# A two-stage layer on one core: expert choice ahead of two routers, the other two as row products on ScalarE and GpSimd

## The reference

```python
x = x + xattn(layernorm(x), fside, ctx)     # per batch: int8-like linear 512->512, silu(gate) * up, linear 256->512
xn = layernorm(x)                           # 2048 tokens
logits = xn @ gate_w.T                      # 8 experts
_, sel = top_k(logits.sum(axis=0), 2)       # two experts for ALL tokens
rw = softmax(logits[:, sel], axis=1)        # a pair of weights for each token
h = gelu(einsum('nd,kdf->knf', xn, w1[sel]) + b1[sel])
y = einsum('knf,kfd->knd', h, w2[sel]) + b2[sel]
x = x + einsum('nk,knd->nd', rw, y)
```

## Time and profile before

| | |
|---|---|
| runs | 820.04, 821.65, 822.15 us (median 821.65) |
| span of the profiled execution | 818.7 us (what lies around it isn't in the profile; the median is 2.95 above the span) |
| PE busy | 771.5 us, 94% |
| DVE, ACT, POOL busy | 477.7, 354.6, 449.7 us |
| chain that ended last | PE 83%, POOL 8%, DVE 3% |
| mean granted clock of TensorE | 0.979 of full |

### The profile page before, as it was taken

The page is one execution under the profiler, slowest core; times in us unless marked ns, Lnnn a source line. Parts: engine busy times, 40 slices in busy tenths (PEclk is TensorE's granted clock), DMA queues, the critical chain, the costliest instruction groups (busy, mean ns, idle before and its releaser), DMA issues.

```text
span 818.7 us, 11342 instructions
## 1 busy us (share of the span) xinstructions
PE 771.5 (94%) x3570; PEld 624.1 (76%) x3577; DVE 477.7 (58%) x669; ACT 354.6 (43%) x660; POOL 449.7 (55%) x497
## 2 busy tenths in 40 slices
PE   5688666999999999999999999999999999999998
PEld 4666455688788888888888888888888888888886
DVE  5999759797754545454545454545454545454545
ACT  3967588743442434343424343434343434242422
POOL 1789997157564646464646464646464646464622
PEclk9899968999999999999999999999999999999999
DMA  9400000301010101010101010101010101010022
GB/s 344 173 2 1 1 0 2 129 1 51 1 52 1 51 0 49 3 50 2 48 4 51 1 45 6 42 9 44 7 41 11 36 15 36 15 32 19 0 103 104
DMA packets 19077, 32.34 MB, mean 39 GB/s; under 512 B 872, under 2 KB 11240, under 8 KB 18160
## 3 DMA queue, kind: packets, MB, share of 16 engines
q1 hardware_dynamic: 18896, 31.98, 11.1%
q10 hardware_dynamic: 160, 0.08, 0.0%
HBM read 27.87 MB, written 4.19 MB: 39 GB/s over the span
## 4 chain that ended last, share of the span: by engine, by line
PE 83%; POOL 8%; DVE 3%; issue 2%; ACT 2%; DMA 1%; ACTq 0%; POOLq 0%; DVEq 0%
PE slot L805 42%; PE slot L792 34%; PE slot L850 3%; POOL wv L366 2%; POOL xf L383 1%; PE slot L667 1%; POOL wv L372 1%; POOL cv L366 1%; PE slot L585 1%; DVE rmax L1226 1%; DMA b_rows<-in_L_ffn_b 1%; POOL rstd L340 1%; POOL h_lo L476 1%; DVE stats L1217 1%; DVE peak_x L1226 1%
## 5 line engine op out<-in xcount | busy, mean ns | idle before, releaser
L792 PE MATMUL slot<-xo,a_hi 128*128 128x512 f32 x840 | 259.1, 390 | 0.0
L1541 DVE SCALAR_TENSOR_TENSOR res<-slot,rw,res 128x512 f32<-128x512 f32 x256 | 178.5, 750 | 130.3 <-PE slot L805 130.2
L1570 DVE TENSOR_TENSOR e<-slot,e 128x512 f32<-128x512 f32 x150 | 103.8, 692 | 173.4 <-PE slot L792 173.3
L805 PE MATMUL slot<-w_hi,h_hi 128*128 128x512 f32 x512 | 201.3, 393 | 0.4 <-POOL h_lo L476 0.4
L805 PE MATMUL slot<-w_lo,h_hi 128*128 128x512 f32 x512 | 199.6, 390 | 0.0
L805 PE MATMUL slot<-w_hi,h_lo 128*128 128x512 f32 x512 | 199.4, 390 | 0.0
L792 PEld LDWEIGHTS slot<-xo,a_hi 128*128 128x128 f32 x840 | 157.4, 188 | 33.3 <-DVE e L1570 0.2
L476 POOL TENSOR_TENSOR h_lo<-e,h_hi 128x512 fp32r<-128x512 f32 x96 | 138.1, 1451 | 55.0 <-ACT e L1104 54.0
L792 PE MATMUL slot<-xo,a_lo 128*128 128x512 f32 x420 | 163.7, 390 | 0.0
L805 PEld LDWEIGHTS slot<-w_hi,h_hi 128*128 128x128 f32 x512 | 96.1, 188 | 25.1 <-POOL h_lo L476 5.6
L476 POOL TENSOR_TENSOR h_lo<-hid,h_hi 128x512 fp32r<-128x512 f32 x32 | 44.1, 1378 | 124.7 <-ACT hid L1104 124.7
(11 more groups left out here) (145 smaller groups left out, 814.5 us busy)
## 6 DMA issues: line engine op xcount, KB each, us to landing
raw<-in_L_ffn_w SPq DMA_DIRECT2D x32, 512.0 KB, 3.4
res<-in_x SPq DMA_DIRECT2D x4, 1024.0 KB, 11.9
wv<-in_fside_BxS2xS SPq DMA_DIRECT2D x4, 1024.0 KB, 12.8
out_x<-res SPq DMA_DIRECT2D x3, 1024.0 KB, 3.9
cv<-in_ctx SPq DMA_DIRECT2D x4, 512.0 KB, 13.1
out_x<-res SPq DMA_DIRECT2D x4, 256.0 KB, 2.7
b_row<-in_L_ffn_b SPq DMA_DIRECT2D x2, 256.0 KB, 4.6
b_rows<-in_L_ffn_b ACTq DMA_DIRECT2D x1, 64.0 KB, 6.0
```

Source lines behind the costliest of these rows:

```text
L792: last = t.matmul(dst, a[:, i, k, :], xo[tp][:, v, k, :], start=(start and n == 0), stop=(n == 3 * H - 1), skip_group_check=True)
L805: last = t.matmul(y_bank[j][:, :], a[:, i, j * P:(j + 1) * P], v[:, f, :], start=(start and n == 0), stop=(not start and n == 2), skip_gro ...
L1541: v.scalar_tensor_tensor(out=r, in0=y_bank[j][:, :], scalar=rw[:, ds(p, 1), n:n + 1].rearrange("p a b -> p (a b)"), in1=r, op0=ALU.mult, o ...
L1570: v.tensor_tensor(dst[:, :], src, other[:, :], ALU.add).then_inc(comb_ready, 1)
```

## The change

Names: T2L and T4L are areas of the tokens' operand tiles that are free at that time; `dot_product(j)` is a 128x512 piece of them.

- The routers of batches 2 and 3 are dropped from PE, with their copies and columns. In their place ACT writes 8 rows of normalised tokens (`dot_row`, 128 tokens x 512 features each), POOL multiplies each with the difference of the two chosen gate rows, which it has made from two rows loaded by DMA (`gate_difference`, `router_products`), and ACT sums each product into a column of `ldiff` with its accumulator (`dot_sum`).
- `expert_sums` comes before the routers of batches 1 and 0. The first up tile comes before the logit columns.
- The logit difference is picked at once, with one product instead of two. The power, its sum with 1 (now on POOL) and the token weights are made in two parts, one for each half.
- The first weights come by two DMAs, and a tile's low weight products come last in each pair of blocks.
- The work around pair 0 on DVE, ACT and POOL is put in another order.

```diff
--- before.py
+++ after.py
@@ -241,6 +249,9 @@
         hid_ready, h_ready = sem("hid_ready"), sem("h_ready")
         y_ready, y_free = sem("y_ready"), sem("y_free")
         stored = sem("stored")
+
+        def dot_product(j):
+            return part(1, (T2L, T4L)[j // 2])[:, (j % 2) * D:(j % 2) * D + D]
 
         x_bank, p_bank, w_bank, y_bank = bank[0], bank[1], bank[2], bank[4:8]
...
-            load_w1(0)
+            first = w1_v[ds(expert[0], 1), 0].rearrange("e p k f -> (e p) k f")
+            sp.dma_start(raw1[:, 0:H, :], first[:, 0:H, :]).then_inc(raw1_top, 16)
+            sp.dma_start(raw1[:, H:KD, :], first[:, H:KD, :]).then_inc(raw1_load, 16)
             load_w2(0)
             expert.append(value_of(1))
+            for k in range(TOPK):
+                sp.dma_start(gate_row[:, k, :], gate_w[ds(expert[k], 1), :].to_broadcast([P, D])).then_inc(gate_load, 16)
...
-            first_pair()
+            def gate_difference():
+                pool.wait_ge(gate_load, 16 * TOPK)
+                link(g.tensor_tensor(gate_row[:, 0, :], gate_row[:, 0, :], gate_row[:, 1, :], ALU.subtract))
+
+            def router_products(b):
+                for j in range(TT):
+                    pool.wait_ge(dot_rows, (b - B // 2) * TT + j + 1)
+                    g.tensor_tensor(dot_product(j), dot_product(j), gate_row[:, 0, :], ALU.mult).then_inc(dot_ready, 1)
+
+            def token_power(tp):
+                pool.wait_ge(lsub_ready, tp + 1)
+                at = slice(tp * HALF, tp * HALF + HALF)
+                link(g.tensor_tensor(lpow[:, at], euler[:, at], lsub[:, at], ALU.pow))
+                g.tensor_scalar(lden[:, at], lpow[:, at], 1.0, None, ALU.add).then_inc(lexp_ready, 1)
+
+            hid_lo(0, 0, 0)
+            token_power(0)
+            hid_lo(0, 0, 1)
+            hid_lo(0, 0, 2)
+            hid_lo(0, 0, 3)
+            gate_difference()
+            router_products(2)
+            router_products(3)
+            hid_lo(0, 1, 0)
+            weight_sums(0)
+            hid_lo(0, 1, 1)
+            token_power(1)
+            hid_lo(0, 1, 2)
+            hid_lo(0, 1, 3)
+            for i in range(7):
+                weight_lo(0, i)
+            down_lo(0, 0, 1)
+            down_lo(0, 1, 0)
...
@@ -774,11 +807,9 @@
             normed2(2, 1)
             normed2(3, 0)
             normed2(3, 1)
+            expert_sums()
             router(1)
-            expert_sums()
             router(0)
-            router(2)
-            router(3)
...
                     if q == 0:
-                        pe.wait_ge(a_ops_ready, 2 * f + h + 1)
+                        pe.wait_ge(a_hi_ready, 2 * f + h + 1)
                     pe.wait_ge(lo_ready[b], h + 1)
                     hi, lo = HI_AT[s][h], LO_AT[s][h]
-                    for k in range(H):
-                        for a, v in ((a_hi, hi), (a_hi, lo), (a_lo, hi)):
+                    for a, v in ((a_hi, hi), (a_hi, lo), (a_lo, hi)):
+                        if q == 0 and a is a_lo:
+                            pe.wait_ge(a_ops_ready, 2 * f + h + 1)
+                        for k in range(H):
                             last = t.matmul(TILE_BANK[n], a[:, 2 * f + h, k, :], xo[q][:, v, k, :],
                                             start=(m == 0), stop=(m == 3 * KD - 1))
                             m += 1
                 last.then_inc(prod_done, 1 if n < 3 else 4)
...
+            up_tile(0, 0)
+            logit_columns(1)
+            logit_columns(0)
+            up_tile(0, 1)
+            up_tile(0, 2)
+            up_tile(0, 3)
+            first_downs(0)
+            for n in range(4):
+                up_tile(1, n)
+            first_downs(1)
+            pe.wait_ge(hid_ready, 8 + 16)
...
@@ -998,8 +1038,11 @@
                 if lo == 0:
                     act.sem_inc(hid_ready, 8)
                     act.sem_inc(e1_ready, 2)
-                    act.wait_ge(raw1_load, 16)
                 for i in range(lo, hi):
+                    if i == 0:
+                        act.wait_ge(raw1_top, 16)
+                    if i == 1:
+                        act.wait_ge(raw1_load, 16)
                     plain_hi(i)
...
@@ -1084,39 +1127,46 @@
             keep_full(2, 0)
             keep_full(3, 0)
             keep_summed(2, 1)
+            keep_summed(3, 1)
             keep_hi(2, 0)
             keep_hi(2, 1)
-            keep_summed(3, 1)
             keep_hi(3, 0)
-            keep_hi(3, 1)
-            keep_logits(0)
             keep_logits(1)
             first_weights(0, 2)
+            keep_logits(0)
             first_weights(2, 4)
             s.activation(gelu_warm[:, :], half[:, 0:1], ACT.Gelu_apprx_tanh)
-            keep_logits(2)
-            keep_logits(3)
-            first_down_weights()
...
+            def dot_sum(b, j):
+                n = b * TT + j
+                act.wait_ge(dot_ready, n - NT // 2 + 1)
+                s.activation(dot_product(j), dot_product(j), ACT.Identity,
+                             accum_out=ldiff[:, n:n + 1]).then_inc(dot_summed, 1)
+
+            def dot_row(b, j):
+                act.wait_ge(nmr_ready[b], 2)
+                if b == B - 1:
+                    act.wait_ge(dot_summed, j + 1)
+                s.activation(dot_product(j), res[:, b * TT + j, :], ACT.Identity, bias=nmr[1][b][:, j:j + 1],
+                             scale=rstd[1][b][:, j:j + 1]).then_inc(dot_rows, 1)
...
-            first_pair()
+            first_bias()
+            gelu_tile(0, 0)
+            first_down_weights()
+            keep_hi(3, 1)
+            gelu_tile(0, 1)
+            gelu_tile(0, 2)
+            gelu_tile(0, 3)
+            dot_row(2, 0)
+            dot_row(2, 1)
+            dot_row(2, 2)
+            dot_row(2, 3)
+            dot_sum(2, 0)
+            dot_row(3, 0)
+            dot_sum(2, 1)
+            dot_row(3, 1)
+            dot_sum(2, 2)
+            dot_row(3, 2)
+            dot_sum(2, 3)
+            dot_row(3, 3)
+            dot_sum(3, 0)
+            dot_sum(3, 1)
+            dot_sum(3, 2)
+            dot_sum(3, 3)
+            gelu_tile(1, 0)
+            operand_hi(0, (T2H, T2L), 4)
+            gelu_tile(1, 1)
+            operand_hi(0, (T3H, T3L), 4)
+            gelu_tile(1, 2)
+            operand_hi(0, (T1H, T1L), 4)
+            gelu_tile(1, 3)
+            operand_hi(0, (T4H, T4L), 4)
+            later_weights()
...
+                dve.wait_ge(logcol_ps, 2)
+                cols = bank[3][:, 0:NT * E].rearrange("p (n e) -> p n e", e=2 * E)
+                link(v.tensor_tensor(between[:, :], onehot[:, 0, :], onehot[:, 1, :], ALU.subtract))
+                link(v.tensor_tensor(picked[:, 0:NT // 2, :], cols,
+                                     between[:, :].unsqueeze(1).to_broadcast([P, NT // 2, 2 * E]), ALU.mult))
+                link(v.tensor_reduce(ldiff[:, 0:NT // 2], picked[:, 0:NT // 2, :], AX.X, ALU.add))
+
+            def logit_maxima(tp):
+                at = slice(tp * HALF, tp * HALF + HALF)
+                v.tensor_scalar(is_top[:, 0, at], ldiff[:, at], 0.0, None, ALU.is_ge)
+                v.tensor_scalar(is_top[:, 1, at], ldiff[:, at], 0.0, None, ALU.is_le)
+                v.scalar_tensor_tensor(out=lsub[:, at], in0=ldiff[:, at], scalar=-1.0, in1=ldiff[:, at],
+                                       op0=ALU.mult, op1=ALU.min).then_inc(lsub_ready, 1)
...
             moments(3, 2)
-            keep_lo(0, 0)
+            normalise_last()
             keep_lo(1, 0)
-            normalise_last()
             token_sums(2)
-            keep_lo(1, 1)
             token_sums(3)
             token_total()
+            keep_lo(1, 1)
+            choose_experts()
+            keep_lo(0, 0)
             keep_lo(0, 1)
-            choose_experts()
-            keep_lo(2, 0)
-            keep_lo(2, 1)
-            keep_lo(3, 0)
-            keep_lo(3, 1)
+            pick_experts()
+            pick_bias()
             first_weights(0, 2)
             first_weights(2, 4)
-            pick_experts()
-            pick_bias()
-            first_down_weights()
+            keep_lo(2, 0)
             pick_logits()
-
-            def token_weights():
-                dve.wait_ge(lexp_ready, 1)
+            logit_maxima(0)
+            keep_lo(2, 1)
-            first_pair()
+            first_down_weights()
+            keep_lo(3, 0)
+            token_weights(0)
+            keep_lo(3, 1)
+            last_operands(0)
+            fourth_operand(0)
+            outputs_of(0, 0, 0)
+            middle_operands(0, 3)
+            outputs_of(0, 0, 1)
+            middle_operands(0, 4)
+            operand_lo(0, 0)
+            operand_lo(0, 1)
+            dve.wait_ge(dot_summed, 2 * TT)
+            logit_maxima(1)
+            operand_lo(0, 2)
+            token_weights(1)
+            outputs_of(0, 1, 0)
+            operand_lo(0, 3)
+            last_operands(1)
+            outputs_of(0, 1, 1)
+            fourth_operand(1)
```

(75 more changed lines are left out.)

70 lines of the change are left out of this document (24 added, 46 removed), and 8 rows, old and new, of the table SLOT_USES.

## The result

The changed kernel takes 830.89 us (median of 4 runs, 829.60 to 832.47) beside 820.99 us before (4 runs on the same chip, 820.04 to 822.15): a ratio of 1.0129, 95% interval 1.0107 to 1.0152. It is slower by about 1.3%. The profiled execution has a span of 827.7 us, 9.0 us more than before.

A forecast was written before the change was run, and what follows sets the result against it. PE was taken to bound the kernel, busy 94% of 818.7 us. 2.1 us won at the start, 11.0 of new PE waits, + 0.3 and - 0.2 gave + 9.0: span 827.7, median 830.7 us, range 822.5 to 835.5.

The forecast's parts named there:

- The sum: Whole kernel: - 2.1 + 11.0 + 0.3 - 0.2 = + 9.0 us of span, to 827.7; 2.95 carried over gives 830.7.
- The start: Up to the fourth up tile's end: two routers and half the logit columns off PE, 2.1 us won (1.0 to 3.5).
- The clock term: At the start: PE's clock 0.50 at the sums, rising during the routers, so 16 passes take 5.1 us.
- The chain of six steps: From the fourth up tile's end (163.7) through ACT, POOL and DVE to the combine freeing the Strassen bank, at 211.4 us.
- step 2: POOL's `h_lo`, gate difference and eight products: 12.5 us, + 5.0 for meetings with DVE's five operand sums, to 182.4.
- step 4: POOL's two `h_lo`, four weight sums, power and add: 7.3 us, + 2.7 for meetings with three `operand_lo`, to 194.3.
- step 3: ACT's last sum and two gelu passes, after POOL's products: 1.9 us, to 184.3.
- PE's waits: Behind the fourth up tile: 11.0 us in pieces of about 3.3, 1.0, 2.6 and 4.1, then another 0.3.
- The clock rival: PE's clock falls in the new gaps, costing 1.5 to 3 us after the last one: 833.0 us, chance 0.22.
- No exclusion: Rival: POOL products hardly collide with DVE, PE waits 1.1 us at the Strassen products: - 1.8 us, 819.8, chance 0.13.
- Half of the meetings: Rival: a blocked DVE or POOL instruction waits 0.5 us, not 1.0: + 3 to + 5, 825.6 us, chance 0.20.
- Routers hidden anyway: Rival at the start: dropping routers does not free PE, 2.1 us won shrink to 1.0; within likeliest case's range.

The follow-up runs named there:

- e4: The kernel before, unchanged, run once more for a second trace: 819.8 us, span 817.9, one run.
- e1: Changed kernel with the first half's nine DVE operand instructions reading their second input from PSUM bank 3 (operand values wrong): 823.35 us.
- e5: Changed kernel with idle matmuls on PE, 15 and 9, before the two halves' third down products: 833.08 us.
- e7: e3 with the same instructions in another order in the DVE, GpSimd and ScalarE queues, whole layer computed: 823.88 us.
- e8: As e7, but eight DVE instructions multiply and add up the rows, gate difference in PSUM, replacing GpSimd's products and ScalarE's sums: 820.77 us.
- e9: e8 with another order of the same instructions on DVE and GpSimd: 820.67 us.
- e2: Changed kernel without GpSimd's gate difference and eight products (second half's routing weights wrong): 826.63 us.
- e3: Changed kernel with GpSimd's products on the residual rows, ScalarE's eight normalised rows dropped, scale and mean put in afterwards: 829.97 us.
- e6: Changed kernel with the edits of e1 and e2 together: 823.11 us.
- e10: e5 with 17 more idle matmuls before the fourth Strassen product of the second pair: 830.53 us.
- e11: e2 with idle matmuls (8, 9 and 17) in PE's three long waits: 826.75 us.

## Why the prediction was right, point by point

- **The sum** was + 9.0 us of span and came out at + 9.0, 830.7 us for 830.89. Two of its parts were off in opposite directions, the start by 2.3 us and what comes behind the fourth tile by 1.8 (another 0.5 came in and behind the loop), so the agreement to 0.2 us is partly luck. So is the step from the span to the median: the 2.95 us carried over are 3.2 here, because the profiled execution is the fastest of the four (829.60 us, 1.9 above its span). The two medians differ by 9.9 us.
- **The start.** Forecast 2.1 us won (1.0 to 3.5), measured 4.4 against the first trace of before and 3.5 against e4's (T = 165.06). (The forecast's own figures, 165.97 and 163.7, are 2.3 apart.) The wait before the sums was as said, 1.62 us for 1.5. The order at the first tile was not: the passes were done at 148.9 and PE waited 0.86 us for the weights, which came about when forecast, 4.3 us behind the copy of the sums for 4.1; the forecast had the passes end last. The clock term was mis-sized: I had it low until the routers, and it was full from 140.1 us on; the 16 passes took 4.24 us for 5.1, and the transposes ended at 142.1 for 143.8. That is one of two cases. Counted from the end of PE's wait at 134 to 135 us, the first down product starts 26.2 us later here and 26.0 to 26.2 in e1, e5, e7, e8 and e9. In e2, e3, e6, e10 and e11 the clock is low once more, for some 3.4 us from 144 or 145 on, the passes take 5.4 us, PE does not wait for the weights, and it is 27.1 to 27.7 us. The two traces of before have 31.3 and 31.1.
- **The chain of six steps** held nearly step by step in its times, in us from the end of the fourth tile, forecast and measured: gelu 1.3, 1.3; products done 18.7, 18.0; second half's first gelu done 20.6, 20.7; power and add done 30.6, 31.1; token weights 33.4, 34.4; the combine that frees the bank 47.7, 48.0. Meetings inside step 2 were 4.1 us for 5.0. In step 4 two weight sums of 1.72 for 0.74 and the power, 2.65 us, met DVE's `operand_lo`: 3.0 us for 2.7. The power alone is what I put between two rows, 1.6 us: it took 1.67 in e5, where DVE was idle beside it. One link was another than forecast: step 3 was to start the second half's gelus behind ScalarE's last sum, and they waited for PE, 0.62 us longer. The forecast did not count that PE's own late start (3.84 us, then 24 passes in 7.24 us, for 5.72 behind e1's wait at full clock) reaches the same gelu. That 20.7 us came out for 20.6 is luck in part; in e5 and e10, where the clock is kept up, the chain does run through the products as forecast.
- **PE's waits.** Forecast 3.3, 1.0, 2.6, 4.1 and 0.3; measured 3.84, none, 2.44, 1.39 and 1.03. The wait of 1.0 for `h_lo` is hidden by the late PE; with the clock kept up it is there, 0.94 us in e5 and 0.97 in e10. The last wait is smaller because the clock fell behind the first ones, and PE came later to the bank: it was busy for 40.4 us up to there instead of its own 36.7. e5 and e10 show that it is the same time under another name: with the clock kept up the last wait is 4.82 us in e5, and e10 ends at 830.5.
- **The clock rival** was right in its mechanism and wrong in its place. The clock fell (0.50 over 171 to 174, 0.76 over 196 to 203), but ahead of a wait, where it costs next to nothing: the 1.5 us that it adds to the 24 passes make PE's path 0.6 us longer than that of the products, which otherwise would be the longer one by 0.9, and the rest comes off the later waits. Behind the last wait, where I had put it, it shows in e5 and costs 2.5 us there at most.
- **No exclusion** was put at 819.8, 1.8 us below before. e1 takes away the meetings of the first half's operand sums and gives 823.35. What is left there is for the most part one wait of 4.03 us for the bank: the second half's operand sums and the bias rows still stand ahead of the combine and still meet GpSimd (3.61 us for two sums of 1.21, 2.60 for two bias rows that take 1.54 in the changed kernel). That rival had no such wait beyond 1.1 us; its 819.8 was too low, or its twelve meetings too few. It also counted back 0.8 us for a late `h_lo`, where the earlier trace rows has 0.41; the wait stayed in every version (0.3 to 0.4 us).
- **Half of the meetings** (825.6) fell with the steps: a blocked instruction did wait about 1 us. **Routers hidden anyway** fell too: the first tile starts 3.8 us earlier, at 149.7, and not at the 152.3 forecast.
- **What no part of the prediction saw** is that the order in the queues, and not the amount of work, is worth 6 us (e7), and that the second half's gelus hang on two paths of nearly one length, so that shortening one of them (e2, e3) gives little.

## What to carry to other kernels

Work that is moved from the bounding engine onto two others has to be priced at those two together where they exclude each other: nine products of 1.3 us cost GpSimd 15.1 us and DVE's operand sums nearly double, and the same products without the turns cost nothing that could be measured (e1 beside e6). Ask, for each side of such a pair, whether an operand can come from PSUM, and where in the queue the pair has room. Look too for a second path to the same point before you judge by leaving one out: without the products 2.9 us came back, since PE's late outputs held the same gelus. And a saving on the bounding engine of 4.85 us is soon spent: its own new wait at the start took half of it.

## What the runs showed of the hardware that was not expected

- The same wait of PE of 3.4 to 3.6 us that ends at 134 to 135 us was followed by very different stretches of low clock: until 145.7 us in the first trace of before, until 144.2 in e4's, until 140.1 in the changed kernel, and in e2 until 141.5 with a second one from 144.9 to 148.3, which begins after the 1.62 us wait for the token total. Of the eleven traces with the new start five (e2, e3, e6, e10, e11) have such a second stretch and six don't, behind the same 1.62 us wait. Nothing in the rows tells which comes.
- A DVE `scalar_tensor_tensor` that adds up its own products costs no more than one that doesn't: they start 0.61 us apart for 512 columns, with a readout of 0.08 under the next, and the outputs of that size 0.68 us apart.
- GpSimd's power waits for DVE as its other instructions do: for the same 8 columns it took 1.67 us in e5 and 2.65 in the changed kernel, where an `operand_lo` ran when it began.
